# A graph layer and a mixture of experts on one core: seven groups' experts move into the gather

## The reference, cut to what matters

```
x1  = x + segment_sum((layernorm(x) @ W)[src] * edge_weight, dst) + b      # 12500 nodes x 256, 200000 edges
y   = layernorm(x1)
logits = mean(y, nodes) @ Wr + br          # one routing decision for all nodes, 8 experts
w   = softmax, cut at the capacity, softmax again; the two largest, softmax
h_e = gelu(y @ W1[e] + b1[e])              # 256 -> 512
o   = sum over the two chosen e of w_e * (h_e @ W2[e] + b2[e])             # 512 -> 256
out = x1 + layernorm(o + y) * gamma + beta
```

## Time and profile before

| | |
|---|---|
| median of 3 runs | 2611.08 us |
| profiled execution: span | 2609.0 us |
| PE busy | 2236.6 us, 86% |
| DVE busy | 1934.6 us, 74% |
| ACT busy | 809.6 us, 31% |
| POOL busy | 1725.3 us, 66% |
| DMA read and written | 224.71 MB, 12.80 MB |

### The profile page before, as it was taken

One profiled execution on the slowest core, in us unless ns is written; L12 is line 12 of the kernel. 1 busy time (PEld: TensorE's weight loads), 2 busy tenths in 40 slices (PEclk: granted clock), 3 DMA queues, 4 the chain that ended last, 5 costly groups with the idle time before them and its releaser, 6 DMA issues.

```text
span 2609.0 us, 43640 instructions
## 1 busy us (share of the span) xinstructions
PE 2236.6 (86%) x11252; PEld 1768.6 (68%) x11253; DVE 1934.6 (74%) x8411; ACT 809.6 (31%) x2323; POOL 1725.3 (66%) x1665
## 2 busy tenths in 40 slices
PE   4799988888888888878788888888888999999998
PEld 3576666666666665665566655565666888888887
DVE  6777777777777777777777777777786666666666
ACT  0001000011121222223333344444456445444543
POOL 6777777777777777777777777777772343344344
PEclk9755566666667677778877898889898999999999
DMA  7633333333333333333333333333332000000000
GB/s 252 205 105 105 105 105 105 105 105 105 105 105 105 105 105 105 105 105 105 105 105 105 105 105 105 105 105 105 104 105 67 17 23 19 25 25 17 25 25 28
DMA packets 104845, 239.16 MB, mean 92 GB/s; under 512 B 26637, under 2 KB 53430, under 8 KB 104696
## 3 DMA queue, kind: packets, MB, share of 16 engines
q0 software_dynamic: 75024, 204.97, 26.9%
q1 hardware_dynamic: 29240, 30.25, 3.6%
q10 hardware_dynamic: 432, 2.40, 0.3%
HBM read 224.71 MB, written 12.80 MB: 91 GB/s over the span
## 4 chain that ended last, share of the span: by engine, by line
PE 43%; DMA 18%; POOL 17%; DVE 12%; issue 9%; ACT 1%; ACTq 0%; DVEq 0%; POOLq 0%
PE ps L480 19%; DMA G<-in_x,SRC 17%; POOL G L380 14%; PE ps L712 7%; PE ps L473 5%; PE ps L732 5%; PE ps L474 2%; PE ps L469 2%; DVE ST L395 2%; PE ps L487 2%; DVE OH L436 2%; POOL Z L755 1%; DVE Z L763 1%; DVE YTl L605 1%; DVE Hlo L721 1%
## 5 line engine op out<-in xcount | busy, mean ns | idle before, releaser
L380 POOL DMA_INDIRECT G<-in_x,SRC x1563 | 1486.4, 951 | 486.5 <-issue 292.5
L480 PE MATMUL ps<-OH,G 128*128 128x128 f32 x6252 | 1283.4, 356 | 310.1 <-DVE OH L436 292.6
L480 PEld LDWEIGHTS ps<-OH,G 128*128 128x128 f32 x6252 | 1041.2, 244 | 540.2 <-DVE OH L436 528.8
L395 DVE BATCH_NORM_STATS2 ST<-G 128x6 f32<-128x256 f32 x1563 | 666.6, 426 | 410.1 <-DMA G<-in_x,SRC 380.6
L436 DVE TENSOR_SCALAR OH<-CST,DL,WR 128x128 f32<-128x128 f32 x1563 | 530.8, 340 | 0.0
L533 ACT ACTIVATE AT<-ps 128x256 f32<-128x256 f32 x98 | 37.5, 383 | 1119.8 <-PE ps L480 1119.6
L401 DVE BATCH_NORM_AGGREGATE MV<-ST 128x2 f32<-128x6 f32 x1563 | 296.9, 190 | 6.8
L716 ACT ACTIVATE Ht<-ps,b1s 128x512 f32<-128x512 f32 (+1 forms) x200 | 136.4, 682 | 309.7 <-PE ps L712 292.4
L732 PE MATMUL ps<-W2h,Hhi 128*128 128x256 f32 x784 | 224.1, 286 | 0.4 <-DVE Hlo L721 0.4
L732 PE MATMUL ps<-W2l,Hhi 128*128 128x256 f32 x784 | 222.0, 283 | 0.0
L732 PE MATMUL ps<-W2h,Hlo 128*128 128x256 f32 x784 | 221.9, 283 | 0.0
(11 more groups left out here) (141 smaller groups left out, 2290.2 us busy)
## 6 DMA issues: line engine op xcount, KB each, us to landing
G<-in_x,SRC POOLq DMA_INDIRECT x1563, 2.7
X<-in_x SPq DMA_DIRECT2D x24, 512.0 KB
out<-Z SPq DMA_DIRECT2D x24, 512.0 KB, 3.0
W1s<-in_W SPq DMA_DIRECT2D x2, 512.0 KB, 4.4
W2s<-in_W SPq DMA_DIRECT2D x2, 512.0 KB, 6.1
DF<-in_dflat SPq DMA_DIRECT2D x1, 782.0 KB, 6.5
DST<-in_dstt ACTq DMA_DIRECT2D x1, 781.5 KB, 6.3
SRC<-in_srct ACTq DMA_DIRECT2D x1, 781.5 KB, 8.6
```

The source lines that it names most:

```text
L380: gathered[s] = put("pool", lambda e: e.indirect_dma_start(out=G[:, s % RING, :], out_offset=None, in_=x, in_offset=bass.IndirectOffsetOnA ...
L395: bn[s] = put("dve", lambda e: e.bn_stats(ST[:, s % 4, :], G[:, s % RING, :]), after=[gathered[s]] + ([aggr[s - 4]] if s >= 4 else []), in ...
L480: ins = e.matmul(ps[:, 0, c * P:(c + 1) * P], G[:, r, c * P:(c + 1) * P], OH[:, r % OHR, :], start=False, stop=True, skip_group_check=True)
```

## The change: what it does

Most of the kernel is rewritten; each engine's program now stands in order in its own block, with waits written out.

- Edges come in reverse order, so node tile 0 is the one with the last 84 nodes and few edges, and tile 97 the one with the first nodes and some 158 edge tiles. NE is 1564, an even number; a node tile begins at a pair of edge tiles.
- x is read once, its rows' statistics are taken (98 tiles, DVE), it is scaled (ACT) and stored to a DRAM buffer `xr_d`. Edge tiles 0 to 95 are still gathered from x with their own statistics, from 96 on from `xr_d`, with none. One gather per edge tile as before, 64 buffers.
- The edge product has the one-hot as stationary operand and G's 256 columns streamed, so the sum stands untransposed; it is copied, transposed twice by PE, multiplied with W. b is added as a 128-row product (two of the rows hold its high and low part). x1 and the normalised, transposed y go to DRAM. These steps run as sections, each tile's steps spread over the sections of the tiles behind it (copy, across, x1, normal, turned); five sections stand behind the last edge.
- Node groups 0 to 6 (28 tiles) go through all 8 experts during the gather, since the choice isn't known yet: 56 units of (group, expert), in f32, weights loaded per unit into one buffer each. The results go to DRAM. 57 events, each a down of one unit and an up of the next, are laid out over the edge tiles of node tiles 18 to 97 in a list computed ahead, and PE compares the edge number with the next event after every second edge tile.
- Behind the gather all 8 W1 lie in SBUF. 18 groups go through the two chosen experts, `up` of one group interleaved with `down` of the former by blocks, b2 as a 128-row product; y needs no transposes. The seven stored groups are combined on DVE (two products each) between them.

```diff
-RING, OHR, NB = 32, 8, 8
+RING, GS, OHR = 64, 16, 8
+FRESH, XBUF = 96, 18
+LOTS = (4, 4, 4, 5, 4, 2, 2)
...
+AHEAD = 7
+UNITS = AHEAD * E
...
+def events():
...
+    room = [max(0.0, 0.75 * slots[t] - 3.5) if t >= 18 else 0.0 for t in range(NT)]
...
+        pre_of = {1 + (len(post) - 3) * a // AHEAD: a for a in range(AHEAD)}
...
+            for s in range(NE):
+                if s >= RING:
+                    e.wait_ge(s_main, s - RING + 3)
+                if s >= GS:
+                    e.wait_ge(gat[s % GS], 16 * (s // GS))
+                if s == FRESH:
+                    for l, lot in enumerate(lots):
+                        e.wait_ge(xs_st[l], 16 * (len(lot) + (lot[-1] == NG - 1)))
+                if s == TABLES:
+                    e.wait_ge(s_tab, tab_ev)
+                e.indirect_dma_start(out=G[:, s % RING, :], out_offset=None, in_=x if s < FRESH else xr_d,
...
+            def fresh(s):
+                n, j = s // 8, s % 8
+                stats(s)
+                newton_steps(n - 1, (4 * j, 4 * j + 1))
+                if s in (12, 13):
+                    for f in range(4 * s - 48, 4 * s - 44):
+                        one_hot(f)
+                if s >= 20:
+                    one_hot(s - 12)
+                stats_end(s)
...
+            for g in range(6, NG):
+                x_stats(g)
...
+                if g < 6 + EARLY:
+                    fresh(g - 6)
...
+            for s in range(EARLY + 1, FRESH):
+                fresh(s)
...
+            def chores(v):
+                e.wait_ge(s_as, v + 1)
+                e.wait_ge(s_at, v + 1)
...
+                    ins = e.transpose(ps[:, TA, c * P:(c + 1) * P], AS[:, c * P:(c + 1) * P], ident)
+                ins.then_inc(s_ta, 1)
+                e.wait_ge(s_pre, v + 1)
...
+                    e.matmul(ps[:, XB, 0:D], AT[:, c * P:(c + 1) * P], Wsb[:, c, :], start=False, stop=True, skip_group_check=True)
+                e.matmul(ps[:, XB, 0:D], ones_r[:, :], b2r[:, :], start=False, stop=True, skip_group_check=True).then_inc(s_w, 1)
+                e.wait_ge(s_xh, v + 1)
+                e.wait_ge(s_yt, v + 1)
...
+                    ins = e.transpose(ps[:, TR, c * P:(c + 1) * P], XH[:, c * P:(c + 1) * P], ident)
+                ins.then_inc(s_tr, 1)
...
+            def begin(v, g):
+                e.wait_ge(s_ohx, v * 2 + 2)
+                e.wait_ge(s_as, v + 2)
...
+            def unit_up(u):
+                e.wait_ge(w1_in, u * 16 + 16)
+                e.wait_ge(yu_in, (u >> 3) * 16 + 16)
+                u4 = e.snap(u * 4)
+                for i in range(4):
+                    e.wait_ge(s_gelu, u4 + (i + 1))
+                    for c in range(2):
+                        ins = e.matmul(ps[:, UP[i % 2], :], W1u[:, c, i * P:(i + 1) * P], YU[:, c, :], start=(c == 0), stop=(c == 1))
+                    ins.then_inc(s_up, 1)
...
+            def unit_down(u):
+                e.wait_ge(w2_in, u * 16 + 16)
+                e.wait_ge(s_gelu, u * 4 + 6)
+                for p in range(2):
+                    e.wait_ge(s_ye, u * 2 + (p + 1))
...
+            def edge(g, r):
+                e.matmul(ps[:, 0, 0:D], OH[:, r, :], Gf[:, bass.ds(g + r * D, D)], start=False, stop=True, skip_group_check=True).then_inc(s_main, 1)
...
+            def event(a, r, g):
+                with e.While(lambda: e.snap(rel) <= r):
...
+                    with e.If(now < UPS):
...
+                        chores(v)
+                        with e.If(now == END):
+                            begin(v, g + (r - 1) * D)
...
+                        with e.If(now > UPS):
+                            unit_down(e.snap(u_r, min_val=0, max_val=UNITS - 1))
...
+                        with e.If(now < DOWNS):
+                            unit_up(e.snap(u_r, min_val=0, max_val=UNITS - 1))
+                    e.reg_mov(rel, e.snap(due) - a)
...
+            for k in range(len(post)):
+                for i in range(HID):
+                    if k + 1 < len(post):
+                        up(k + 1, i)
+                    down(k, i)
```

More of the change, by code:

```diff
@@ L57, in gnn_ffn, with tiles, slot, sections @@
-def gnn_ffn(nc, x, dflat, srct, dstt, wt, W, b, Wr, br, W1, b1t, W2, b2, gamma, beta, cst, iota_e, out):
+GT = 4
+NG = (NT + GT - 1) // GT
+AHEAD = 7
+UNITS = AHEAD * E
+HID = 2 * F // P
+HB = 4
+VIRTUAL = 4
+FINAL = NT - 1 + VIRTUAL
+END, EXTRA, UPS, BOTH, DOWNS = range(5)
+def tiles(g):
+    return range(g * GT, min((g + 1) * GT, NT))
+def slot(t):
+    return len(tiles(t // GT)) - 1 - t % GT
+def sections():
+    copied = [v if v < NT - 1 else NT - 1 if v == FINAL else None for v in range(FINAL + 5)]
+    out, waiting, turned = [], [], None
+    for v in range(FINAL + 5):
+        x1 = copied[v - 2] if v >= 2 else None
+        root = x1 // GT if x1 is not None and (x1 == NT - 1 or x1 % GT == GT - 1) else None
+        waiting += tiles(root) if root is not None else []
+        xh = waiting.pop(0) if waiting else None
+        out.append({"copy": copied[v], "across": copied[v - 1] if v else None, "x1": x1, "root": root, "xh": xh, "yt": turned})
+        turned = xh
+    assert not waiting and turned is None
+    return out
@@ L130, in gnn_ffn @@
[L130 to L141, removed]
@@ L163, in row @@
[L163 to L172, removed]
@@ L191, in gnn_ffn @@
-        flag = put("dve", lambda e: e.tensor_copy(FLAG[0:1, 0:1], ps[0:1, 7, 0:1]), after=[fs], inc="dve_flag")
[L195 to L198, removed]
+        early = At()
+        SRC = early("SRC", [P, NE], i32)
+        WR, DL, ND = early("WR", [P, NE + 1]), early("DL", [P, NE]), early("ND", [P, NE])
+        WT = WR[:, 1:NE + 1]
@@ new lines, in gnn_ffn @@
+        s_zr, s_zg, s_fin, s_b1s = sem("pool_zr"), sem("dve_zg"), sem("dve_fin"), sem("dve_b1")
+        out_st, out_last = [sem(f"out{k}") for k in range(3)], sem("out_last")
+        ends = range(0, FRESH + 1, 8)
+        lots = [range(sum(LOTS[:k]), sum(LOTS[:k + 1])) for k in range(len(LOTS))]
+        lot_of = [k for k, lot in enumerate(lots) for _ in lot]
+        assert len(lot_of) == NG
+        batches = list(zip(ends, ends[1:]))
+        batch_of = [n for n, (a, z) in enumerate(batches) for _ in range(a, z)]
@@ new lines, in _ @@
+            xh_at, root_at = {}, {}
+            for s in (s_as, s_at, s_pre, s_xh, s_yt):
+                e.sem_inc(s, 1)
+            for s in (s_gelu, s_ye):
+                e.sem_inc(s, 2)
+            e.wait_ge(s_init, 2)
+            e.wait_ge(s_tab, tab_rows)
+            e.wait_ge(s_set, SETS)
+            e.wait_ge(cst_in, 16)
+            match(1)
+            for l in range(len(lots)):
+                seed_x(l)
+                scale_x(l)
+            for t, _, kind, n in EVENTS:
+                if kind in (BOTH, DOWNS):
+                    unit_out(n - 1)
+                if kind in (UPS, BOTH):
+                    unit(n)
+                if kind in (END, EXTRA):
+                    section(n)
@@ new lines, in slots @@
+            def slots(a, g, n):
+                for r in range(n):
+                    if r % 4 == 0:
+                        e.wait_ge(s_oh, a + (r + 4))
+                    edge(g, r)
+                    if r % 2 == 1:
+                        event(a, r, g)
+            with e.Fori(0, NE // OHR) as i:
+                a = e.snap(i * OHR)
+                g = e.snap((i & (RING // OHR - 1)) * (OHR * D))
+                e.reg_mov(rel, e.snap(due) - a)
+                slots(a, g, OHR)
+            a = NE // OHR * OHR
```

1542 lines of the change are left out of this document (977 added, 565 removed).

## The result

The changed kernel takes 2445.03 us (median of 4 runs, 2443.69 to 2445.92), the kernel before beside it 2610.88 us: a ratio of 0.9363, 95% interval 0.935 to 0.9376, or 166 us less. The forecast was 2475 with a range of 2430 to 2585. The profiled execution has a span of 2443.8 us, against 2609.0.

The account below looks back on a forecast made before the run. The prediction took POOL's 1.2555 us per gather to bound the gather stage and PE the tail. Last edge product at 2024 us plus a 446 us tail gave a 2470 us span, forecast as 2475 us, range 2430 to 2585.

Parts of the forecast that it names:

- forecast A: Whole kernel: POOL's gather rate holds, PE ends up to 50 us behind, 2440 to 2500 us; chance 0.48.
- Gather cadence, second wait: Gather stage: POOL still takes 1.2555 us per gather, and the second wait now in front of each costs 0.
- Rival E: Gather stage: the second wait slows each gather by 0.1 us, 2630 us in all; chance 0.03.
- Start stall: Start: POOL stalls 22 us (10 to 50), 17 of them because one-hot 8 comes only near 115 us.
- The 5 us for DMA: Start: 5 us added to the stall because DMA's 139 us come close to gather 96 at 148 us.
- PE's lag: Gather stage: PE needs 99% of POOL's time, so the last edge product ends 25 us after the last landing.
- Event tests: Gather stage: PE's event-register test after every second edge stays hidden; 782 exposed tests would add 84 us.
- DVE's relief: Gather stage: statistics and Newton steps taken off DVE are cover, not path, since DVE follows POOL; no gain counted.
- Seam, tail, end: After the last edge: seam 24 us, half clock 2, PE's tail work 401, bubbles 8, end 11; 446 us.
- The 8 us of bubbles: Tail: 8 us added to PE's 401 us of work there.
- Rival B: PE bounds the gather stage (event tests, edges nearer 0.515 us) or DVE bounds the tail, 2500 to 2606 us; chance 0.34.
- rival D: Gather stage: units leave gaps, PE's mean clock falls well below full, 2740 us at rate 0.86; chance 0.07.

Follow-up runs that it names:

- fresh_all: Changed kernel with 1560 instead of 96 edge tiles gathered from x itself, their statistics and Newton steps on DVE again: 2609.75 us, ratio 0.9999.
- half_units: Changed kernel with half of the products (one half of the contraction) left out of every unit in the gather stage: 2440.7 us in one run.
- start: Changed kernel with ACT serving node tile 0 after the fifth lot of x and 104 edge tiles gathered from x: 3264 us on the slower chip.
- fresh_oh16: As fresh_all, but 16 one-hot buffers instead of 8 and 17 buffers for x instead of 18: 3345 us on the slower chip, 2469.5 us when run again elsewhere.
- bias2: Changed kernel with 2 rows instead of 128 in both bias products: 3260 us on the slower chip, 2454.3 us when run again elsewhere.
- no_pool: Changed kernel without all but one element of each of POOL's two large additions in the tail: tail 421.8 us, on the slower chip.

## Why the prediction was right

The mechanism of forecast A holds: POOL's rate is kept, PE fits just below it, the tail loses seven groups. The forecast was 30 us too long, nearly all of it in prices that were set too high. By its own steps:

- **Gather cadence, second wait.** 1.2555 predicted, 1.2534 measured; gaps stay at 0.30 us with two waits. Rival E is out. By the rule of the Trainium skill (SBUF — State Buffer, Who interferes with whom) that a VectorE instruction in a two-port mode blocks GpSimd's descriptor writing, the forecast had left the emptier DVE at most 0.01 us a gather. One gather takes 949 ns in the changed kernel with DVE busy 1027 us and 949 ns in fresh_all with DVE busy 1802: in the steady stage nothing of it is seen.
- **Start stall.** 22 predicted, 12.4 measured in two holes. One-hot 8 as a cause was right, but came at 103.85 and not near 115; ACT's order, which stood in no step, was just as late. The 5 us for DMA did not come. 10 us of the error.
- **PE's lag.** This decided, and every piece was priced too high. The stretch from 1986.98 to 1993.89 has 16 edges: 0.432 us each (0.453 predicted). A unit is 7.00 + 6.87 = 13.9 (14.3, with waits 14.7). Chores take 2.3 us, for instance from 208.01 to 210.32 (2.8). From 400 to 1990 us PE was busy 1503 of 1590 us, 95% (375.67, 370.08, 381.18, 192.28 and 184.05 in stretches of 400, 400, 400, 200 and 190), where the sum had 99. The predicted 25 us behind the last landing, or 28 behind the last gather's start, were 10: 18 us of the error.
- **Event tests.** Bursts of 16 edges contain 8 tests and show no gap, so the Trainium skill's 108 ns for a compare-and-branch (Advanced Engine Details and Errata, Control Flow Timing) is not seen in them, as the sum had it; exposed they would have cost 84 us. Where PE's program goes over to other work it does pause for nothing that the profile shows ("issue"): 34 times and 19.3 us in all ahead of units, 28 times and 10.7 us ahead of a tile's chores.
- **DVE's relief.** The step "this is cover, not path: DVE follows POOL" failed. The kernel before fits it (DVE's statistics waited 380.6 us for gathers), but PE never left the edges there for as long as a unit. Beside units of 14 us and with 8 one-hot buffers it is path, by fresh_all 165 us of it. The sum didn't suffer, since it took DVE as light; but I would have forecast the same for the change without its scaling, and been 165 us off.
- **Seam, tail, end.** Seam 22.9 us (24). Tail's PE time 2016.76 to 2431.7, 415 us (2 + 401 + 8); group 23.00 (22.9). End 12.1 (11). DVE in the tail 346.6 us (347), which is luck in part, since its pieces differ: 949 ns for the low half instead of 680, 0.61 and 0.48 us for the two finishing steps instead of 0.55. The 8 us of bubbles came out as 12, PE's 415 us less 17 groups of 23.0 and one of 11.7. Together 450 against 446.

Of the 30 us, then, 10 are the stall, 2 the cadence, 18 the lag; 4 come back in the tail, and 4 lie in what was added to the span to come to the median (5 us, where 1.2 would have done).

Rival B was near: one group more, and PE is the bound. Its own mechanisms (event tests, edges at 0.515) did not occur. Of rival D only the direction is seen, in half_units: idle PE, lower clock. D did not occur: from 400 to 1990 us PE was busy 95% at clock 0.98.

## What to carry to other kernels

When work is moved into a stage that another engine bounds, the sum of PE's time is not enough: a block of 14 us on one engine asks for rings around it that last longer than the block (here 8 one-hots lasted 10 us of POOL's rate, 16 last 20), or the engines behind it stop and must catch up at their own pace. Look for in-order engines whose next instruction waits for a buffer while useful ones are queued behind it. And a long ring hides lateness: with a ring of 64 tiles PE was 68 us behind and the bounding engine's rows looked perfect, so read the last consumer's end, not the producer's.

## What had not been expected of the hardware

One chip ran every kernel slower: the kernel before took 3091 us there (ratios above are each against the kernel before on the same chip), and start took 3264, ratio 1.0567 (1.0528 to 1.0605), fresh_oh16 3345, bias2 3260. The changed kernel itself did not run there, but start and bias2 differ from it by little, so there the change would most likely be a loss. The tail was as fast as elsewhere (428.1 us); all of the difference lies before it. A stretch of start there, and PE's waits over its whole span:

```profile
800.00:1200.00 400.00, 306.23 (x1094) 219.82 (x1092) 75.39 (x234) 166.78 (x512) 225.09 (x236) 0.87 0.47 139
```
```profile
PE ps L1257 <- DVE OH L971: 237.4, 42, 66.9
PE ps L1257 <- issue: 98.8, 76, 7.8
...
PE ps L1226 <- issue: 77.9, 18, 13.5
```

In the changed kernel the first of these is 73.1 us and the second 25.1. Single products take what they take elsewhere (7.17 and 7.03 us for a unit's halves), but between them PE waits for nothing that the profile shows, up to 13.5 us at a time. PE's program loops and branches in the gather stage, and that invites an explanation; but DVE, whose instructions stand one behind the other without a loop, stops there too, and long before PE's loop begins. The same instruction in the changed kernel and in start:

```profile
30.95 0.25 DVE L888 CAST FROW<-ps 1x98 int32<-1x98 f32 x1 [0.88 <-PE ps L1189]
```
```profile
51.25 0.25 DVE L890 CAST FROW<-ps 1x98 int32<-1x98 f32 x1 [20.92 <-remote]
```

In start all of PE's products ahead of it had ended by 31.2 us. DVE stood 20.9 us all the same, as it did in fresh_oh16, bias2 and no_pool on that chip, and the first edge product came at 125.8 us instead of 74.4. What holds the engines up there was not tested, and the cause stays open.

Between products of 128 rows, a product of 2 rows cost PE 0.33 us more here than one of 128: fewer rows were not cheaper. And a DVE instruction with two inputs from SBUF is up to half as long again beside POOL's large additions (949 ns over the whole tail, 999 from 2100 us on, against 674 without them), while POOL's mean gather took 949 ns whether DVE was busy 1027 or 1802 us.
